# CoPE attention on one core: table selection by four groups of 32 rows, scores built one slot later, and comparison, subtraction and rounding moved behind the start of the next selection

## What is computed

```python
def cope(query, attn_logits, pos_emb):
    npos_max = pos_emb.shape[-1]                 # 64
    gates = jax.nn.sigmoid(attn_logits)
    pos = jnp.flip(jnp.cumsum(jnp.flip(gates, axis=-1), axis=-1), axis=-1)
    pos = jnp.minimum(pos, npos_max - 1)
    pos_ceil = jnp.ceil(pos).astype(jnp.int32)
    pos_floor = jnp.floor(pos).astype(jnp.int32)
    logits_int = jnp.einsum('bhqd,dn->bhqn', query, pos_emb)
    logits_ceil = jnp.take_along_axis(logits_int, pos_ceil, axis=-1)
    logits_floor = jnp.take_along_axis(logits_int, pos_floor, axis=-1)
    w = pos - pos_floor
    return logits_ceil * w + logits_floor * (1.0 - w)
...
logits = jnp.einsum('bhqd,bhkd->bhqk', Q, K) / jnp.sqrt(jnp.asarray(d, Q.dtype))
scores = jax.nn.softmax(logits + cope(Q, logits, pos_emb), axis=-1)
out = jnp.einsum('bhqk,bhkd->bhqd', scores, V)
```

## Time and profile before

| | us |
|---|---|
| median of 3 runs | 15340.84 (15337.57 to 15372.86) |
| profiled execution, its own time | 15370.8 |
| its span, first to last instruction | 15369.1 |
| CoPE stage, 4714 to 14600 of the span | 9886 |
| busy: PE, DVE, ACT, POOL | 12799.3, 7438.2, 4440.7, 6509.8 |

### The profile page before, as it was taken

How to read it: one execution, slowest core, us unless ns; L and a number is a source line. 1 busy time by engine, 2 the same in 40 slices (tenths; PEclk the granted TensorE clock), 3 DMA queues, 4 the chain that set the end, 5 groups by cost and what they waited for, 6 DMA issues and landing times. The chain is left out here.

```text
span 15369.1 us, 176674 instructions
## 1 busy us (share of the span) xinstructions
PE 12799.3 (83%) x57462; PEld 8566.0 (56%) x57462; DVE 7438.2 (48%) x13140; ACT 4440.7 (29%) x7890; POOL 6509.8 (42%) x5384
## 2 busy tenths in 40 slices
PE   8878999999667888888888888888888888888845
PEld 3554333333445666666666666666666666666622
DVE  0112222232225666666666666666666666666633
ACT  0111222222113333333333333333333333333310
POOL 0000000000005666666666666666666666666600
PEclk9888988888777888888888888888888888888866
DMA  3111000000113333333333333333333333333223
GB/s 81 44 46 29 21 19 20 20 20 20 59 57 70 81 81 81 81 81 81 81 81 81 80 80 80 81 81 79 81 81 80 82 80 80 81 81 81 69 69 100
DMA packets 1037896, 1029.79 MB, mean 67 GB/s; under 512 B 738306, under 2 KB 845570, under 8 KB 972306
## 3 DMA queue, kind: packets, MB, share of 16 engines
q1 hardware_dynamic: 964114, 1020.70, 27.7%
q10 hardware_dynamic: 73728, 8.42, 0.4%
HBM read 817.83 MB, written 210.76 MB: 67 GB/s over the span
## 5 line engine op out<-in xcount | busy, mean ns | idle before, releaser
L916 PE MATMUL c_pickps<-c_table,c_hot 128*128 128x112 f32 x16384 | 3464.9, 388 | 563.3 <-DVE c_over L1207 541.9
L916 PEld LDWEIGHTS c_pickps<-c_table,c_hot 128*128 128x128 f32 x16384 | 3296.3, 265 | 667.6 <-DVE c_over L1207 569.3
L1297 POOL TENSOR_TENSOR c_total<-c_total,c_over 128x384 f32<-128x384 f32 (+3 forms) x3584 | 3284.0, 916 | 476.8 <-DVE c_over L1207 197.5
L1184 DVE COPY_PREDICATED c_pickps<-c_upper,c_pickps 128x256 f32<-128x256 uint32 (+1 forms) x1024 | 799.0, 826 | 3349.3 <-PE c_pickps L916 3349.3
L1297 POOL TENSOR_TENSOR c_total<-c_total,c_middle 128x1024 f32<-128x1024 f32 x512 | 1210.0, 2363 | 2853.6 <-DVE c_middle L1198 2853.6
L1264 POOL IOTA c_digitrow<- 1x128 f32 x1 | 0.3, 255 | 4614.4 <-POOLq L65 4614.4
L1049 ACT ACTIVATE c_over<-c_place,c_thresholds 128x384 f32<-128x384 f32 (+3 forms) x3584 | 1589.2, 525 | 0.0
L1207 DVE TENSOR_TENSOR c_over<-c_over,c_pickps 128x384 f32<-128x384 f32 (+3 forms) x3584 | 1407.1, 452 | 0.0
L1032 ACT ACTIVATE c_place<-c_gateps 128x512 f32<-128x512 f32 x1024 | 611.4, 597 | 2674.2 <-PE c_gateps L889 2674.1
L510 DVE TENSOR_REDUCE a_max<-a_peakps 128x1 f32<-128x1024 f32 x512 | 627.0, 1225 | 1202.7 <-PE a_peakps L442 1202.7
L464 PE MATMUL a_outps<-a_probs,a_v 128*128 128x512 f32 x2048 | 1201.5, 716 | 0.3 <-DVE a_outT L522 0.3
(11 more groups left out here) (213 smaller groups left out, 14832.8 us busy)
## 6 DMA issues: line engine op xcount, KB each, us to landing
c_hot<-t_digits SPq DMA_DIRECT2D x512, 1024.0 KB
t_tables<-c_tablesb SPq DMA_DIRECT2D x256, 256.0 KB, 5.1
c_table<-t_tables SPq DMA_DIRECT2D x1024, 56.0 KB, 2.3
c_kb<-t_kb SPq DMA_DIRECT2D x256, 128.0 KB, 6.1
t_digits<-c_anchorrows SPq DMA_DIRECT2D x128, 256.0 KB, 2.4
a_q<-t_qa SPq DMA_DIRECT2D x128, 128.0 KB, 2.4
a_k<-t_ka SPq DMA_DIRECT2D x128, 128.0 KB, 2.5
c_ka<-t_kb SPq DMA_DIRECT2D x128, 128.0 KB, 5.6
```

Source lines behind the costliest of these rows:

```text
L916: mm = nc.tensor.matmul(pick_ps[:, h // 4, 0:WIDTH, r * 8:(r + 1) * 8], hot[t % 2][:, h, :], table[s][:, :, :, t * 16 + h].rearrange("p l ...
L1184: ins = nc.vector.copy_predicated(pick_ps[:, :, at:at + width, :], far.unsqueeze(2).to_broadcast([128, 4, width, 32]), pick_ps[:, :, at + ...
L1297: nc.gpsimd.tensor_tensor(a, a, b, ALU.add).then_inc(s_add, 1)
```

## The change

The selection no longer runs as 16 matmuls of 128 rows and 112 columns, but as 64 of 32 rows and 28 columns. Group `g` takes rows 32g to 32g + 31 of `hot` and of `table` and writes to a PSUM bank of its own, bank g of the four of `pick_ps`. The order of queries within a quad's table and anchor tiles changes to suit (`keep_table`, and `near`, whose anchor write is now contiguous). On PE, `logits` of slot n - 1 now comes at the start of slot n, `values` trails by two slots, and both stand ahead of `add_cope`. On DVE, `top` and `top_row` come later among the products, and `less`, `compare` (now for slot n + 2) and `near` stand behind the last product, which is what the next pick waits for; only for the first pick of a quad `compare` stands ahead of it, in slot 3. `norm` on ACT and `recip` on DVE trail by two slots too. On SP, the load of V is issued after a later `load_hot`.

```diff
@@ pick
                 for h in range(16):
                     if h == 8 and turn is not None:
                         turn_anchor(turn)
-                    r = h % 4
-                    mm = nc.tensor.matmul(pick_ps[:, h // 4, 0:WIDTH, r * 8:(r + 1) * 8], hot[t % 2][:, h, :],
-                                          table[s][:, :, :, t * 16 + h].rearrange("p l m -> p m l"), start=True, stop=True)
+                    for g in range(4):
+                        rows, lanes = slice(32 * g, 32 * g + 32), slice(2 * g, 2 * g + 2)
+                        mm = nc.tensor.matmul(pick_ps[:, g, 0:WIDTH, h:32:16], hot[t % 2][rows, h, :],
+                                              table[s][rows, lanes, :, t * 16 + h].rearrange("p l m -> p m l"),
+                                              start=True, stop=True)
                 mm.then_inc(s_pickps, 1)
@@ PE, the slot
-            def pieces(i, t, at):
-                if t == 0 and at < 5 and not final(i):
-                    gates(i + 1, at)
-                elif t == 1 and at < 3 and not final(i):
-                    gates(i + 1, at + 5)
+            def piece(i, t, at):
+                if t < 2 and at < 4 and not final(i):
+                    gates(i + 1, 4 * t + at)
                 elif t == 3 and at < 2 and not final(i, 2):
                     tables(i + 2, at)
...
+                    if one:
+                        if t:
+                            logits(i, s, t - 1)
+                        else:
+                            logits(i - 1, 1 - s, 3)
+                    if two:
+                        if t < 2:
+                            values(n - 2, x, 1 - s)
+                        elif t == 2:
+                            values(n - 2, x, s, i)
+                        else:
+                            values(n - 2, x, s)
+                    if one:
                         add_cope(n - 1, 1 - x)
-                    if ahead:
-                        pieces(i, t, 0)
-                    if behind:
+                    piece(i, t, 0)
+                    if one:
                         turn_peak(n - 1, 1 - x)
...
                         bases(n - 1, 1 - x)
...
-                    logits(i, s, t)
-                    if ahead:
-                        pieces(i, t, 3)
...
+                    piece(i, t, 2)
+                    piece(i, t, 3)
+                    if t == 2 and ahead:
+                        places(i + 1, 1 - s)
                     if t < 3:
                         pick(i, s, t + 1, i + 1 if t == 2 and ahead else None)
@@ DVE, near
-                nc.vector.tensor_scalar(anchor[:, :].rearrange("p (t l h) -> p t h l", t=4, l=8),
-                                        rounded[:, :].rearrange("p (t h l) -> p t h l", t=4, l=8), EIGHTS, None, ALU.subtract).then_inc(s_anchor, 1)
+                nc.vector.tensor_scalar(anchor[:, :], rounded[:, :], EIGHTS, None, ALU.subtract).then_inc(s_anchor, 1)
@@ DVE, the slot
                     mux(i, s, t)
-                    if behind:
+                    for k in range(2):
+                        product(i, s, t, k)
+                    if two:
+                        recip(n - 2, x)
+                    product(i, s, t, 2)
+                    if one:
                         top(n - 1, 1 - x)
-                    product(i, s, t, 0)
-                    if behind:
+                    for k in range(3, 5):
+                        product(i, s, t, k)
+                    if one:
                         top_row(n - 1, 1 - x)
-                    product(i, s, t, 1)
-                    if behind:
-                        less(n - 1, 1 - x)
-                    for k in range(2, 5):
-                        product(i, s, t, k)
-                    if t < 3:
-                        compare(n + 1, 1 - x, 2 * i + (t + 1) // 2 + 1)
-                    elif ahead:
-                        compare(n + 1, 1 - x, 2 * i + 3)
                     for k in range(5, PRODUCTS):
                         product(i, s, t, k)
-                    if t == 2 and ahead:
+                    if t == 3 and ahead:
+                        compare(4 * i + 4, 0, 2 * i + 3)
+                    if one:
+                        less(n - 1, 1 - x)
+                    if t < 2:
+                        compare(n + 2, x, 2 * i + 2)
+                    elif t == 2 and ahead:
                         near(i + 1, 1 - s)
-                    if behind:
-                        recip(n - 1, 1 - x)
+                    elif t == 3 and ahead:
+                        compare(4 * i + 5, 1, 2 * i + 3)
```

More of the change, by code:

```diff
@@ L1001, in step @@
                         pick(i + 1, 1 - s, 0)
-                    if ahead:
-                        pieces(i, t, 5)
             for n in range(2):
@@ L1014, in _ @@
             quads(pe, step)
+            logits(last, 1, 3)
+            values(4 * last + 2, 0, 1)
             add_cope(4 * last + 3, 1)
@@ L1072, in step @@
                     n, x = 4 * i + t, t % 2
[L1073 removed]
+                    one = not (isinstance(n, int) and n < 1)
+                    two = not (isinstance(n, int) and n < 2)
                     def aside(at):
[L1076 to L1079 removed]
+                        if t < 2 and ahead:
+                            gate(i + 1, 1 - s, 4 * t + at)
                         elif t == 3 and at < 2 and not final(i, 2):
                             keep_table(i + 2, at)
+                    if two:
+                        if t > 1:
+                            norm(i, s, t - 2)
+                        else:
+                            norm(i - 1, 1 - s, t + 2)
                     aside(0)
                     aside(1)
[L1085 removed]
+                    if one:
                         keep_base(n - 1, 1 - x)
                     aside(2)
[L1088 removed]
+                    aside(3)
+                    if one:
                         expo(n - 1, 1 - x)
[L1090 to L1095 removed]
+                    if t == 2 and ahead:
+                        keep_anchor(i + 1)
                     if t < 3:
@@ L1099, in step @@
                         past(i + 1, 1 - s, 0)
-                    if t == 2 and ahead:
-                        keep_anchor(i + 1)
-                    if behind:
-                        if t:
-                            norm(i, s, t - 1)
-                        else:
-                            norm(i - 1, 1 - s, 3)
+                    if t < 2 and ahead:
+                        lift(i + 1, 1 - s, t)
             for n in range(2):
@@ L1118, in _ @@
             quads(act, step)
+            norm(last, 1, 2)
             keep_base(4 * last + 3, 1)
```

55 lines of the change are left out of this document (19 added, 36 removed).

## The result

| | before | after |
|---|---|---|
| median, us | 15356.85 (4 runs, 15337.57 to 15404.43) | 16212.15 (4 runs, 16133.53 to 16217.51) |
| ratio, 95% interval | | 1.054 (1.0505 to 1.0575) |
| quad, mean of 123, us | 77.3 | 83.5 |
| slots 0, 1, 2, 3, us | 18.1, 17.6, 20.5, 21.1 | 21.1, 19.5, 23.9, 19.0 |

The kernel is 5.4% slower; 15790 us was forecast, within 14800 to 16500. A slot here runs from the end of one pick to the end of the next, by the trace's records of the pick's last matmul; slot t ends with the pick of the tile behind tile t.

What follows compares the result with a forecast made beforehand. The CoPE stage was taken as bound by a ring of DVE's work and the pick, 77.2 us a quad. At low clock 38.0 + 18.2 + 24.5 = 80.7, times 128 is +448: 15790 us, range 14800 to 16500.

Steps and rivals of the forecast that it cites:

- 3.8 us at 2.4 GHz and 6.8 at 1.2: Time of one four-group pick on PE, from 32 steps of weight loading shared by the groups; before, 6.33 us at 1.00.
- The step of 0.209 us at 1.2 GHz: One full-height record of `values` at low clock, taken as a pick's step; 0.114 us at 2.4 GHz.
- Rival 2: Four groups share a step only in part: pick 5.4 us at the high clock, 16660 us; chance 0.15.
- 0.70 was forecast: Granted clock of the CoPE stage after the change, near 0.70 against 0.86 before.
- the change takes away the work under which it rose: PE's clock rose under the old picks; without them, 1.2 GHz was expected for most of each slot's front.
- Rival 1: The clock stays high in the CoPE stage and the kernel gets faster: 14550 us; chance 0.25.
- the sum for the high clock: Quad at high clock: 38.0 + 15.3 + 17.7 = 71.0 us, 6.2 less than before, -794 us in all.
- 8.5, with 3.4 for `add_cope`: Us at 1.2 GHz for `logits`, `values` and `add_cope` ahead of `top`; 4.6 us at 2.4 GHz.
- the terms: The quad's parts at low clock: slots 3 and 0 38.0 us, slot 1 18.2, slot 2 24.5.
- three comparisons that were to wait some 2, 6 and 5 us: DVE waiting for the DMA of selection tiles in slots 3 and 0.
- 80.7: Us a quad in the CoPE stage with low clock in front, 3.5 more than 77.2.
- the rest costs nothing: POOL's work, `keep_table` and V's later load in the CoPE stage were taken to add no time.

Runs made afterwards that it cites:

- two_groups: The changed kernel with the pick in two groups of 64 rows and 56 columns instead of four of 32 and 28: 15385.06 us.
- four_in_two: two_picks with four groups of 32 rows instead of two of 64 in each quad's second and third tile: 15981.99 us.
- two_picks: three_picks with the fourth tile of a quad also selected in one group of 128 rows, only second and third in two of 64: 15191.75 us.
- before_loop4: The kernel before with four quads in a turn of the loop instead of two, same work and order: 15428.02 us, 1.0054 of before.
- three_picks: two_groups with the first tile of each quad selected in one group of 128 rows: 15436.06 us.
- both halves by themselves: Against the kernel before: the new order with the old pick, ratio 1.0101; the four-group pick in the old order, ratio 1.0616.
- groups_alone: The kernel before with the four-group pick and its layouts, in the old order: 16276.61 us, 1.0616 of before.
- filler_in_pick: The changed kernel with four extra constant matmuls a tile inside the pick, one ahead of every fourth lane set: 18070.84 us.
- filler: The changed kernel with four extra constant matmuls a tile on PE ahead of the wait for the peak: 16668.04 us.
- anchor_filler: three_picks with four extra constant matmuls in the fourth tile's pick, where PE waits for the anchors: 15326.59 us.

## Why the prediction was right, and what it left out

**The pick.** 3.8 us at 2.4 GHz and 6.8 at 1.2 were forecast from the weight loads that groups share. Measured: 3.77, and 3.40 for half of one. (The step of 0.209 us at 1.2 GHz comes out of `values` only with a tail twice as long, 0.28 us, and with that tail the sum is 7.0, not 6.8.) Rival 2, groups that share only in part, is out. two_groups shows the reading behind it: 64 records in 3.81 us, 32 steps again.

**The clock.** 0.70 was forecast and 0.70 measured; four_in_two shows that the picks cause it. That the figure itself was hit is luck in part, for the prediction has no sum behind it. The step "the change takes away the work under which it rose" was right in its sign. What I had not seen is how regular it is. The clock falls in every slot. For the picks of the first three tiles the fall lies, at the median, within 1 us of the pick's end; for the fourth tile's it lies 5.8 us ahead of the end, in the wait for the anchors. It is back 9 to 11 us behind the pick's end. Rival 1, 14550 us at a high clock, needed a form of pick that keeps it there; two_picks at 0.88 comes nearest, and even so takes 15191.75 us. From `mux` to `mux` its slots 3 and 0 take 39.1 us, slot 1 takes 15.8 and slot 2 takes 21.3, where the sum for the high clock has 38.0, 15.3 and 17.7: it is slot 2 that stays long, and its fourth tile is picked in the long form.

**What the low clock costs.** `logits`, `values` and `add_cope` follow one another from 9009.91 to 9019.11, 9.2 us; forecast were 8.5, with 3.4 for `add_cope`, which takes 3.76. `top` waits 2.82 us for them here and 2.4 in the mean of all slots; forecast were 2 to 3. four_in_two takes 790 us more than two_picks with picks of the same length (3.9 and 3.8 us for its second and third tile at the median, against 3.81); its gaps are 80 us of that.

**The slots.** In the quad shown, slots 3 and 0 take 38.38 us (38.0 forecast), slot 1 takes 17.69 (18.2) and slot 2 22.52 (24.5): the terms hold to 2 us. Of the three comparisons that were to wait some 2, 6 and 5 us for selection tiles, the first doesn't wait and the others wait 4.59 and 5.13. Over all quads it is 40.5, 19.1 and 23.9 from `mux` to `mux`, 83.5 in all against 80.7.

**What was missing.** The step that failed is "the rest costs nothing": the pick's 16 matmuls became 64, and nothing in my sum asked where their instructions come from. The change's body has 2880 matmul and weight records a turn, before it was 1344; with the fetch PE idles 3.8 us a turn, 238 us of the 422 between 15790 and 16212. That the gaps come from the length is shown by before_loop4, where nothing but the length changed and they appeared, and by two_picks, where they are gone, and each gap of the change holds an instruction packet. How much of the 238 us would be left if it vanished from the change is not settled: in three_picks 138 us less of gaps brought nothing.

The Trainium skill ("Runtime: NRT & Kernel Launch", Instruction fetch mechanics) says that TensorE holds 2048 instructions, fetched in blocks of 256, and that a taken branch to a place outside what is held stalls. The trace agrees in its pattern: most stalls stand at the branch, and two_picks with 1600 records a turn has none, three_picks with 1728 has 15 and two_groups with 1856 has 59. The runs thus put the edge between 1600 and 1728 records; that instructions without a record make up the rest to 2048 is not shown. Nor do the gaps simply grow with the length: four_in_two with 2112 records has 27, and before_loop4 with 2688 has 11 in 31 turns, where the change has 71 in 62. That PE has more slack there would explain it, but is a guess. The same section of the Trainium skill says that crossing a block is mostly hidden. The trace agrees: the stage of the change has 844 instruction packets and 71 gaps.

The rest of the 422 us can be placed, though not all of it explained. 109 us come from which executions were profiled: that of the kernel before is 30 us above its median, that of the change 79 below its own. Between the profiled executions and the forecast for them, 15819, there are 314 us, and they stand at the turns. Cut from the `mux` of one slot 3 to the next, the 62 stretches without a turn take 81.0 us in the mean (slots 3 and 0 38.6, slot 1 18.6, slot 2 23.7): there the forecast of 80.7 holds. The 62 with a turn take 86.0. Of the 5.0 us more, 3.8 are the gaps; the other 1.2 are not traced.

That both halves by themselves made the kernel slower, and groups_alone by more than I expected, means that no half of the diff was a gain hidden by the other.

Not settled is what in a four-group pick lets the clock fall: thin rows, few columns for each load of weights, the load of weights itself, or the scattered writes of single elements. Two groups differ from four in several of these at once.

## What to carry to other kernels

A busy time that shrinks by 1119 us can make a kernel slower by 855. Before TensorE's work is cut finer, look at what runs behind it at the high clock, and price it at the low one. Take the form of the pick tile by tile: where its neighbours wait anyway (here for DMAs), the long dense form can be the better one, because it keeps the clock: with it for the fourth tile too, two_picks is 244 us under three_picks. And count the instructions in the body of a loop: the row of the instruction queue in the profile, 28 packets or 857, tells whether the body is fetched again at every turn. It doesn't tell how long PE waits for it: two_groups and three_picks have 583 and 582 packets, but 59 and 15 gaps.

## What the hardware showed unexpectedly

- Two groups of 64 rows and four of 32 take the same time for the same work, 3.81 and 3.77 us, but leave the stage at 0.79 and 0.70 of the clock.
- A 128-row matmul between matmuls of row groups costs more than by itself: 0.50 us each at the high clock in filler_in_pick, 0.34 in filler, where four in a row take 1.36 us. Four of them stretched a pick from 3.8 to 7.4 us, part of it at the lower clock.
- Four constant matmuls in a wait of TensorE (anchor_filler) raised the clock of the 8 us behind it from 0.50 to 0.71 in the mean of all quads and made the kernel 0.6% faster than without them.
- A loop body that is fetched again at every turn (857 instruction packets against 28) left TensorE idle for 3.8 us a turn, although its instructions make up 0.4% of the DMA time.
